# Attention scores of a gated two-block kernel: six bf16 terms on 99 rows, or two float32r parts on 64-row halves

## The reference, cut to what matters

```python
# block 1, attention, from x (b, 256, 512) and ctx (b, 512, 512)
q = layernorm(x) @ w_q.T          # 32 heads of 16
k, v = ctx @ w_k.T, ctx @ w_v.T   # 8 groups of 16, each serving 4 heads
s = q_h . k_g / sqrt(16)          # (256, 512) per head, masked keys -> -inf
x = x + tanh(g_xattn[1]) * (softmax(s) @ v) @ w_out.T
# then: h = quant(layernorm(x)); y = quant(relu(h@wg.T)**2 * (h@wu.T)) @ wd.T
x = x + tanh(g_ffn[1]) * y
```

## Time and profile before

| What | us |
|---|---|
| median of 3 runs | 262.46 |
| the three runs | 261.26, 263.61, 262.46 |
| span of the profiled execution | 259.9 |
| first score (L782) to end of the last `pv` (L831) | 59.0 to 226 |
| end of the loads before step 0 that a matmul waits for | 36.2 |

### The profile page before, as it was taken

The page is one execution under the profiler, slowest core; times in us unless marked ns, Lnnn a source line. Parts: engine busy times, 40 slices in busy tenths (PEclk is TensorE's granted clock), DMA queues, the critical chain, the costliest instruction groups (busy, mean ns, idle before and its releaser), DMA issues.

```text
span 259.9 us, 4692 instructions
## 1 busy us (share of the span) xinstructions
PE 244.6 (94%) x1472; PEld 120.2 (46%) x1472; DVE 206.9 (80%) x592; ACT 190.2 (73%) x317; POOL 124.0 (48%) x176
## 2 busy tenths in 40 slices
PE   8488989799999999999999999999999999998984
PEld 8443449647433343474244365434334244444431
DVE  3789676669898479767999995989888974999995
ACT  3536598659798998587698388998969988546631
POOL 7005920466332207455888662558978987100000
PEclk9959999999999999999999999999999999999999
DMA  6999962660497850004500830720000000000004
GB/s 190 358 372 358 405 267 63 142 132 4 111 316 221 153 161 3 0 1 112 74 0 0 308 140 0 153 32 1 5 0 0 3 0 0 3 1 0 3 0 161
DMA packets 9154, 27.63 MB, mean 106 GB/s; under 512 B 1514, under 2 KB 4122, under 8 KB 7882
## 3 DMA queue, kind: packets, MB, share of 16 engines
q1 hardware_dynamic: 8698, 21.63, 28.9%
q0 software_dynamic: 288, 5.70, 6.3%
q10 hardware_dynamic: 144, 0.00, 0.0%
HBM read 23.87 MB, written 3.41 MB: 105 GB/s over the span
## 4 chain that ended last, share of the span: by engine, by line
PE 71%; DVE 7%; DMA 7%; SPq 6%; ACT 6%; issue 3%; DVEq 0%; ACTq 0%
PE bank L804 12%; PE bank L831 11%; PE bank L782 10%; DMA big<-in_ctxT 7%; PE bank L807 7%; PE bank L854 5%; PE bank L872 5%; PE bank L724 4%; PE bank L714 4%; PE bank L790 4%; PE bank L760 2%; PE bank L839 1%; DVE fs L1317 1%; SPq L470 1%; PE bank L749 1%
## 5 line engine op out<-in xcount | busy, mean ns | idle before, releaser
L1252 DVE CUSTOM_DVE_ANT_0 junk<-bank,maskb 128x512 bf16<-128x512 f32 x128 | 83.8, 687 | 13.5 <-PE bank L782 12.6
L1026 ACT ACTIVATE big<-bank 128x512 f32<-128x512 f32 x128 | 75.1, 596 | 15.1 <-PE bank L804 10.8
L590 POOL TENSOR_TENSOR big<-big,product 128x512 int32<-128x512 int32 x48 | 61.6, 1285 | 33.6 <-ACT big L1026 33.2
L804 PE MATMUL bank<-qst,kst 99*128 99x512 bf16 x128 | 49.0, 383 | 0.2
L782 PE MATMUL bank<-kst,qst 96*128 96x512 bf16 x128 | 47.8, 381 | 0.6 <-DVE mx L1252 0.4
L831 PE MATMUL bank<-big,vp 128*32 128x512 f32 x256 | 30.6, 598 | 0.0
L807 PE MATMUL bank<-ident_b,maskb 128*128 128x512 bf16 x80 | 30.4, 380 | 0.0
L600 POOL TENSOR_TENSOR mx<-mx 128x4 f32<-128x4 f32 x64 | 16.0, 249 | 22.0 <-DVE mx L1252 19.6
L782 PEld LDWEIGHTS bank<-kst,qst 96*128 96x128 bf16 x128 | 12.5, 99 | 21.4 <-issue 11.0
L804 PEld LDWEIGHTS bank<-qst,kst 99*128 99x128 bf16 x128 | 12.4, 97 | 20.6 <-ACT big L1026 7.2
L1009 ACT ACTIVATE qst<-bank 3x512 bf16<-3x512 f32 x32 | 18.9, 590 | 0.9
(11 more groups left out here) (190 smaller groups left out, 413.2 us busy)
## 6 DMA issues: line engine op xcount, KB each, us to landing
stage_w<-in_w_down POOLq DMA_DIRECT2D x1, 2816.0 KB, 11.6
stage_w<-in_w_gate SPq DMA_DIRECT2D x1, 2752.0 KB, 15.7
stage_w<-in_w_up POOLq DMA_DIRECT2D x1, 2752.0 KB, 14.8
qst<-q_parts SPq DMA_DIRECT2D x18, 128.0 KB, 4.8
big<-in_ctxT SPq DMA_DIRECT2D x8, 256.0 KB, 9.8
q_parts<-parts SPq DMA_DIRECT2D x12, 128.0 KB
big<-in_ctx SPq DMA_DIRECT2D x4, 256.0 KB, 4.7
x<-in_x SPq DMA_DIRECT2D x4, 256.0 KB, 5.9
```

The source lines that it names most:

```text
L590: nc.gpsimd.tensor_tensor(p, p, keep[:, nt, KEEP_ST.index(i):KEEP_ST.index(i) + 1, :].broadcast_to([P, HG, P]), ALU.mult).then_inc(kept, 1)
L804: i = mm(o[:, :], kst[0:KM, b, g, s * P:(s + 1) * P], qst[0:KM, tile % 2, g * HG:(g + 1) * HG, :], start=True, stop=by_keep(c, s))
L1026: fn(pt[:, c % 4, s, :], o[:, :], ACT.Exp).then_inc(drain(stage), 1)
L1252: v.tensor_tensor_reduce(junk[:, j % 2, :], o[:, :], maskb[:, tb(c // NG)[1], :], 1.0, HIDE, ALU.add, ALU.max, mx[:, c % 3, 0, hh:hh + 1]) ...
```

## The change

Query and key are split in two float32r parts (ScalarE writes the upper, VectorE the lower). Three products of parts need 48 rows, with three rows for the maxima 51. They are put in a 64-row half: groups 0 to 3 at partition 0, groups 4 to 7 at partition 64, and the chunks run in the order 0, 4, 1, 5, ... so that halves alternate. `s` multiplies all 51 rows, so the maxima's rows are set to zero by a DMA first (`z_dram`). Every `t` gets its mask from two 64-row matmuls of 256 columns each; `maskx` is `maskb` with its halves exchanged, made by two DMAs. `keep` and `keepT` are gone. The lags are 12 and 26, `woT` is loaded in eight pieces to follow the order of groups, `vp` has 24 columns for each group. `FILL` stays, but for keepT.

```diff
-NTERM = 6
-Q_TERMS = ((0, 1, 2), (3, 4), (5,))
-NPICK = 2
-KS = NTERM * DH
-KM = KS + 3
+HALF = P // 2
+NM = 3
+M_ROW = 2 * DH
+KM = 3 * DH + NM
+Q_ROWS = ((0, DH), (M_ROW + NM,))
+K_ROWS = ((0, M_ROW + NM), (DH,))
+GROUPS = (0, 4, 1, 5, 2, 6, 3, 7)
...
-LAG_T = 11
-LAG_PV = 25
+LAG_T = 12
+LAG_PV = 26
...
-    ("ln0q", 2), ("y0", 0, 1), ("y0", 0, 2), ("ln0r", 2), ("mask",), ("k", 1, 2), ("load_ctx", 4), ("fabs", 0, 0),
+    ("ln0q", 2), ("y0", 0, 1), ("y0", 0, 2), ("ln0r", 2), ("mask",), ("load_maskx",), ("k", 1, 2), ("load_ctx", 4), ("fabs", 0, 0),
...
-    ("vcopy", 0), ("qpick", 0, 0), ("r", 2), ("qpick", 0, 1), ("fround", 0, 1), ("fclamp", 0, 0), ("fclamp", 0, 1),
+    ("vcopy", 0), ("qpick", 0), ("r", 2), ("fround", 0, 1), ("fclamp", 0, 0), ("fclamp", 0, 1),
...
+def place(g):
+
+    return g // (NG // 2) * HALF, g % (NG // 2)
...
-        kst = sb("kst", [P, B, NG, SK], BF16)
-        qst = sb("qst", [P, 2, NH, P], BF16)
+        kst = sb("kst", [P, B, NG // 2, SK], F32R)
+        qst = sb("qst", [P, 2, NH // 2, P], F32R)
...
-        early = qst[:, 1, :, :].rearrange("p a b -> p (a b)").bitcast(F32)
+        zeros = stage_w[0:NM, 0:SK].rearrange("p (a s) -> p a s", a=1)
+        early = tern[1][:, 0:4 * D * 2].bitcast(F32)
...
         def _(sp):
 
+            sp.wait_ge(zeros_ready, 1)
+            sp.dma_start(z_dram.rearrange("p (a s) -> p a s", s=SK), zeros.broadcast_to([NM, NG // 2, SK])).then_inc(zeros_stored, 16)
...
-                        sp.dma_start(kst[KS:KM, b, :, :], minus.broadcast_to([KM - KS, NG, SK])).then_inc(kones_ready, 16)
+                        for r in (M_ROW, HALF + M_ROW):
+                            sp.dma_start(kst[r:r + NM, b, :, :].bitcast(F32), minus.broadcast_to([NM, NG // 2, SK])).then_inc(kones_ready, 16)
+                elif kind == "load_maskx":
+                    sp.wait_ge(mask_ready, SQ // P)
+                    sp.dma_start(maskx[0:HALF, :, :], maskb[HALF:P, :, :]).then_inc(maskx_loaded, 16)
+                    sp.dma_start(maskx[HALF:P, :, :], maskb[0:HALF, :, :]).then_inc(maskx_loaded, 16)
...
                 elif kind == "load_wo":
-                    sp.dma_start(woT[:, :, :], woT_in).then_inc(ld_wo, 16)
+                    for c, g in enumerate(GROUPS):
+                        sp.dma_start(woT[c % 2 * HALF:(c % 2 + 1) * HALF, c // 2, :],
+                                     woT_in[g % 2 * HALF:(g % 2 + 1) * HALF, g // 2, :]).then_inc(ld_wo, 16)
...
+                    if kind == "qsplit":
+                        h0 = 0 if i else HG
+                        for r in (M_ROW, HALF + M_ROW):
+                            sp.wait_ge(zeros_stored, 16)
+                            sp.dma_start(qst[r:r + NM, i % 2, h0:NH // 2, :].bitcast(F32),
+                                         z_dram[:, h0 * P:NH * P // 2]).then_inc(done, 16)
...
         def _(pool):
+            nc.gpsimd.memset(zeros, 0.0).then_inc(zeros_ready, 1)
...
-                elif kind == "keep":
-
-                    c, i = stage[1:]
-                    if KEEPS.index(stage) == 0:
-                        wait_drained(pool, ("keepT",))
-                    wait_drained(pool, ("t", c, i))
-                    p = pt[:, c % 4, i, :].bitcast(I32).rearrange("p (h q) -> p h q", h=HG)
-                    nt = c // NG % (SQ // P)
-                    nc.gpsimd.tensor_tensor(p, p, keep[:, nt, KEEP_ST.index(i):KEEP_ST.index(i) + 1, :].broadcast_to([P, HG, P]),
-                                            ALU.mult).then_inc(kept, 1)
...
                 elif kind == "qpick":
...
-                        i = mm(o[0:KS, :], pick[:, g, part, :, :], parts[0:32, part, :], start=(part == 0),
-                               stop=(part == 2))
-                    i.then_inc(fill(stage), 1)
+                    mm(o[0:HALF + KM, :], pick[:, 0, :], parts[:, 0, :], start=True, stop=False)
+                    wait_drained(pe, ("q", 0))
+                    mm(o[0:HALF + KM, :], pick[:, 1, :], parts[:, 1, :], start=False, stop=True).then_inc(fill(stage), 1)
...
                     o = free_bank(pe, stage)
-                    mm(o[:, :], qst[0:KS, tile % 2, g * HG + hh, :], kst[0:KS, tb(tile)[0], g, :], start=True,
+                    mm(o[:, :], qst[r:r + KM, tile % 2, g * HG + hh, :], kst[r:r + KM, tb(tile)[0], g, :], start=True,
                        stop=True).then_inc(fill(stage), 1)
...
                     o = free_bank(pe, stage)
-                    i = mm(o[:, :], kst[0:KM, b, g, s * P:(s + 1) * P],
-                           qst[0:KM, tile % 2, g * HG:(g + 1) * HG, :], start=True, stop=by_keep(c, s))
-                    if not by_keep(c, s):
-                        i = mm(o[:, :], maskb[:, nt, s * P:(s + 1) * P], ident_b[:, :, :], start=False, stop=True)
+                    i = mm(o[:, :], kst[r:r + KM, b, g, s * P:(s + 1) * P],
+                           qst[r:r + KM, tile % 2, g * HG:(g + 1) * HG, :], start=True, stop=False)
+                    oh = o[:, :].rearrange("p (h n) -> p h n", h=HG)
+                    for half in range(2):
+                        same = maskb if half * HALF == r else maskx
+                        i = mm(oh[:, :, half * HALF:(half + 1) * HALF], same[r:r + HALF, nt, s * P:(s + 1) * P],
+                               ident_h[r:r + HALF, :, :], start=False, stop=(half == 1))
...
-                    fn(qs[:, :], o[:, :], ACT.Copy, scale=scale).then_inc(float_copied, 1)
-                    fn(parts[:, 0, :], o[:, :], ACT.Copy, scale=scale).then_inc(drain(use), 1)
-                    act.wait_ge(remainder_ready, n + 1)
-                    fn(parts[:, 1, :], qs[:, :], ACT.Copy).then_inc(part2_ready, 1)
+                    fn(parts[:, 0, :], o[:, :], ACT.Copy, scale=1.0 if kind == "ksplit" else DH ** -0.5).then_inc(upper_ready, 1)
...
-                    dve.wait_ge(float_copied, n + 1)
-                    wait_drained(dve, (kind[0], t))
-                    v.tensor_tensor(qs[:, :], qs[:, :], parts[:, 0, :], ALU.subtract).then_inc(remainder_ready, 1)
-                    dve.wait_ge(part2_ready, n + 1)
-                    v.tensor_tensor(parts[:, 2, :], qs[:, :], parts[:, 1, :], ALU.subtract).then_inc(part3_ready, 1)
+                    o = wait_filled(dve, (kind[0], t))
+                    dve.wait_ge(upper_ready, n + 1)
+                    v.scalar_tensor_tensor(out=parts[:, 1, :], in0=o[:, :], scalar=1.0 if kind == "ksplit" else DH ** -0.5,
+                                           in1=parts[:, 0, :].bitcast(F32), op0=ALU.mult,
+                                           op1=ALU.subtract).then_inc(drain((kind[0], t)), 1)
```

More of the change, by code:

```diff
@@ L55 @@
 VW = 32
+VS = 24
 NCHUNK = NT * NG
@@ L245, in psum_uses @@
                 take(stage[:2], now, pool)
[L246 removed]
+        elif kind in ("warm", "vt", "csum", "q1T", "r", "p", "hT", "oT", "aT", "f1T", "f2T", "fscale", "qpick"):
             take(stage, now, pool)
@@ L361, in gated_blocks_kernel @@
         ld_ffn = [sem(f"ffn_loaded{w}") for w in range(3)]
-        parts_stored = [sem(f"parts_stored{i}") for i in range(3)]
+        parts_stored = [sem(f"parts_stored{i}") for i in range(2)]
+        zeros_ready = sem("zeros_ready")
+        zeros_stored = sem("zeros_stored")
+        maskx_loaded = sem("maskx_loaded")
         k_stacked = [sem(f"k_stacked{b}") for b in range(B)]
@@ L452, in gated_blocks_kernel @@
         LN_H = [s for s in SCHEDULE if s[0] in ("ln1", "ln2") and s[2] == LN_PARTS - 1]
-        KEEPS = [s for s in SCHEDULE if s[0] == "keep"]
         SPLITS = [s for s in SCHEDULE if s[0] in ("ksplit", "qsplit")]
@@ L501, in _ @@
                     dram, done = (k_dram[i], k_stacked[i]) if kind == "ksplit" else (q_dram[i], q_stacked[i])
-                    for part in range(3):
+                    for part in range(2):
                         if part == 0:
+                            sp.wait_ge(upper_ready, n + 1)
+                        else:
                             wait_drained(sp, (kind[0], i))
-                        else:
-                            sp.wait_ge((part2_ready, part3_ready)[part - 1], n + 1)
@@ new lines, in _ @@
+                    for part in range(2):
+                        sp.wait_ge(parts_stored[part], 16 * (n + 1))
+                        for half in range(2):
+                            c0 = half * NG // 2 * (SK if kind == "ksplit" else HG * P)
+                            if kind == "ksplit":
+                                for r in K_ROWS[part]:
+                                    r += half * HALF
+                                    sp.dma_start(kst[r:r + DH, i, :, :].bitcast(F32), dram[part, :, c0:c0 + NG // 2 * SK]).then_inc(done, 16)
+                            else:
+                                for r in Q_ROWS[part]:
+                                    r += half * HALF
+                                    sp.dma_start(qst[r:r + DH, i % 2, h0:NH // 2, :].bitcast(F32),
```

(12 more changed lines are left out.)

170 lines of the change are left out of this document (58 added, 112 removed), and 1 row of the table FILL.

## The result

Four runs of the changed kernel took 311.31 to 317.14 us, median 313.67; the kernel before took 260.84 to 263.61, median 261.86, on the same chip. The ratio is 1.195, interval 1.188 to 1.203: slower, by 52 us, and far outside the range of 256 to 279. Medians here are of all runs of a kernel; the ratios leave out runs over 1.5% above its quickest, which also had the lower granted clocks, and so leave out the traced run of the changed kernel (317.14 us, mean clock 0.913; its other three 0.918 to 0.928).

A forecast was written before the change was run, and what follows sets the result against it. TensorE was taken as the bound, 164 of the loop's 167 us. Span 259.9 + 3.1 (first score) + 2.0 (clock) - 2.4 (loop) = 262.6, plus 2.6 to the median: 265.2 us; range 256 to 279, the forecast's own 262 to 269.

The forecast's parts named there:

- Masks, +10.5: In the loop, two 256-column mask matmuls for all 128 steps instead of 80, 0.218 us per step: +10.5 us.
- float32r at 0.218: In the loop's matmuls, 512 float32r columns taken as a single pass of 0.218 us; a double pass would cost 0.43.
- Overlap, -24: In the loop, each score hides under its step's weights' matmul and masks in the opposite half: -24 us, at most -27.9.
- R2: In the loop, row halves take turns, each score costing 0.218 us again: 287 us, 275 to 280 part hidden; chance 0.15.
- Borders, 99 x 0.09: In the loop, 99 changes between 64-row and 128-row work cost 0.09 us each: +8.9 us, at least 0.
- The lags ... add a step at the end, +0.6: At the loop's end, lags of 12 and 26 add a step: +0.6 us, about cancelled by the reliefs.
- The clock: Before the loop, half clock behind TensorE's 5.0 us gap: +2.0 us, up to 3.4, or 0 without a fall.
- Part 2 (b): In SyncE's early loads, the wait for the mask delays k(0,2) to 41.7, +5.5 us with the zeros' delay included.
- Part 2 (a): At the head of SyncE's queue, the memset and store of zeros move the early chain by +1.35 us.
- Reliefs of ScalarE and VectorE: In the splits, two of three ScalarE passes and one of two VectorE passes go; about cancelled against other small terms.
- (1): Sign in SyncE's queue: first load near 2.1 us, and no load issued until the mask at about 35.
- (4): Sign in the loop: a start 0.1 us late at each border between 64-row and 128-row work.

The follow-up runs named there:

- e1: The changed kernel with SyncE's store of zeros moved back to the ones' rows, and the mask's copy put behind load_wq: 300.8 us, ratio 1.149.
- e3: The changed kernel with the load order of e1 and query and key parts in bfloat16 instead of float32r (scores less precise): 284.2 us, ratio 1.086.
- e12: e3 with the lags of the kernel before, 11 and 25 instead of 12 and 26: 270.2 us, ratio 1.031.
- e4: The kernel before with all 128 masks added by full-height bfloat16 matmuls and no GpSimd multiplications: 271.0 us, ratio 1.037.
- e9_two_halves: e8_51_rows with the weights' matmul and its masks in the upper row half, opposite the score; terms left out: 271.5 us, ratio 1.029.
- e8_51_rows: e4 with masks as two 64-row matmuls and scores and weights' matmuls cut to 51 rows, all in one half; terms left out: 283.2 us, ratio 1.084.
- the control: e4, all in full height, with lags 12 and 26 instead of 11 and 25; also called e15_lag12_full_masks: 280.0 us, ratio 1.069.
- e5: The kernel before with only a wait for the mask added in SyncE's queue, where the change copies it; nothing copied: 267.9 us, ratio 1.026.
- e11_zeros_late: The changed kernel with only the store of zeros and its memset moved later; the mask's copy still stops the queue: 310.2 us, ratio 1.191.
- e10: The kernel before with the split reading the bank on both ScalarE and VectorE, ScalarE's float32 copy gone: 260.25 us, ratio 0.995.
- e15_lag12_full_masks: e4, all in full height, with lags 12 and 26 instead of 11 and 25: 280.0 us, ratio 1.069.
- e7_split_t: e1 with each float32r weights' matmul of 512 columns split in two of 256 columns: 305.4 us, ratio 1.158.
- e14_lag11_float32r: e1 with lags 11 and 25 instead of 12 and 26, still in float32r: 297.7 us, ratio 1.122.

## Why the prediction was wrong, step by step

The medians make a chain from the changed kernel to the one before: order of the loads -12.9 (e1), float32r to bfloat16 -16.6 (e3), lags -14.0 (e12), halves to full height with the old split +0.7 (e4), masks -9.5 (before). By the runs in the ratios it is -14.8, -14.7, -14.1, +1.0 and -9.5. Each difference holds its share of low clock.

The loop alone, forecast at -2.4 us, came out at +43.1 in the traces: 16.4 of low clock, and at full clock 8.0 for float32r (e1 to e3), 10.6 for the lags (e3 to e12), -1.0 for halves against full height (e12 to e4) and 9.1 for the masks (e4 to before). Two terms that I had at nothing or next to it, the clock in the loop and the lags, make 27 of them; the other large miss is that the overlap less the borders, -15.1 in the forecast, gave 1.0.

- **Masks, +10.5:** measured 9.5. Right.
- **float32r at 0.218:** the term that I took from the low end. It is 0.34 (94.98 to 95.33), between my two bounds. I had read float32's doubled time as two passes of 0.218; no row shows passes, and 0.34 fits neither one nor two of them. Worth 8 us of the loop at full clock (188.9 - 180.9), and 17 in time with the clock.
- **Overlap, -24:** right in kind (starts 0.01 apart), 20 at full clock in e9_two_halves, where 108 scores have a neighbour to hide behind. The changed kernel has 85 such scores; I had taken 128. R2, turns for the halves, is excluded; its 287 us came closest for other reasons.
- **Borders, 99 x 0.09:** a real term, too small: 0.20 a pair in bfloat16, 0.21 + 0.08 around a float32 block. With 52 blocks the latter would be 15 instead of 9, an estimate; e8_51_rows, with bfloat16 halves, shows 11.4. Less overlap and dearer borders together bring halves and full height out even: e12 and e4 have loops of 170.3 and 171.3.
- **"The lags ... add a step at the end, +0.6":** the step that failed outright. It is 9.0 in the control, and 14.0 from e3 to e12. I had counted what a lag adds at the end of the loop, and not that it shifts two stages against everything written at fixed steps in FILL.
- **The clock:** taken as 2.0 us behind one gap. That gap and its fall are there (e5: 5.0 us idle, half clock). In the loop I had none, and it is 16 us: the largest term of all, and its cause stays open beyond the fact that it comes with two halves side by side. No row of before warned of it: its loop has 1.00 throughout.
- **Part 2 (b), the wait:** +4.15 without (a), and 2.0 for the clock, 6.2 together; e5_wait_mask took 6.7 more, k(0,2) at 40.8 for my 41.7 with (a). Right.
- **Part 2 (a), +1.35 for the zeros:** the first load came 1.48 later, as worked out, but I let the shift travel unchanged. TensorE then waited 2.92 us for ctxT at 30.55, the clock was 0.50 from 30.6, and the mask was written at 39.38, against 33.41 in e11_zeros_late and 32.89 before, so the wait of (b) ended 6 us later. First score 7.0 us later by the zeros alone (71.35 against 64.4).
- **Reliefs of ScalarE and VectorE:** cancelled by guess. The shorter split is worth 1.2 us in e10, with a first score 1.6 us earlier, and e1_order has its first score 1.7 us before the old one.

Of the marks set in advance, (1) and (4) came true in kind, and so did (2) but for the first score, which came at 71.35 and not at 62 to 65; (3) came true in the starts but not in the step, 0.63; and by (5) a loop over 172 made it wrong.

## What to carry to other kernels

Before two row halves are set side by side, run a pair of them and look at the granted clock, the price of each type for 512 columns, and the start of the next full-height matmul: here the three took all that the overlap gave. Count also how many pairs the order lets stand side by side. A lag or any shift between stages in a hand-written order is a change of its own; measure it alone, with all else as before. A wait in the queue of loads costs what stands behind it, and a small delay at its head can grow with each wait that it meets: here 1.5 us at the first load, 6 at the mask, 7 at the first score.

## What the runs showed that I had not expected

- The granted clock falls to 0.50 while TensorE is busy without a gap (98.95 to 112.60), in kernels with two 64-row halves side by side. Mean clocks of runs: 0.913 to 0.928 in the changed kernel, 0.943 to 0.968 in e9_two_halves, 0.985 to 0.994 in full height with the old lags. The full-height e15_lag12_full_masks has a fall as well, at 85.2 us, but behind the 2.13 us of idle time shown above.
- float32r costs 0.34 us for 512 columns, in two pieces as in one; bfloat16 0.22, float32 0.43.
- Entering half height behind a float32 block costs 0.21 us, leaving it 0.08.
- Two halves hide a score only where the order puts the right neighbour beside it: 108 of 128 scores in the best case here, 85 in the changed kernel.
- In e7_split_t and e14_lag11_float32r the float32r kernels had the lowest clocks of all, down to 0.889 and 0.898. Why float32r halves should have more of it than bfloat16 ones is open.
